# Two wide attentions of a decoder on one core: softmax sums inverted by way of DRAM, weight loads and clearing moved behind pairs

## What is computed

```python
def L0_xattn(mask, encodings, ...):      # 64 sequences, E=64, T=256, 8 heads of 8
    q, k, v = split(mask.T @ w_in.T + b_in)
    scores = q k^T / sqrt(8), kept where |i - j| <= 64
    o = softmax(scores) v
    o = (o @ w_out.T + b_out).T
    return einsum('nit,io->not', relu(o) * encodings, w_ct) + b_ct

def L1_xattn(q, k, v):                   # k = v = the context, q = layernorm(x)
    return softmax(q_h^T k_h / sqrt(8)) v_h      # 8 heads of 8, 256 x 256 scores
```

## Time and profile before

| | |
|---|---|
| median of 3 runs | 2706.45 us (2706.38 to 2707.54) |
| the profiled execution's own time, its span | 2692.82 us, 2690.8 us |
| mean granted TensorE clock | 0.914 |
| busy: PE, DVE, ACT, POOL | 2236.3, 1829.1, 1153.3, 892.3 us |
| first wide attention | about 373 to 1021 us |
| causal attention | about 1423 to 1733 us |
| second wide attention | about 1747 to 2290 us |

### The profile page before, as it was taken

How to read it: one execution, slowest core, us unless ns; L and a number is a source line. 1 busy time by engine, 2 the same in 40 slices (tenths; PEclk the granted TensorE clock), 3 DMA queues, 4 the chain that set the end, 5 groups by cost and what they waited for, 6 DMA issues and landing times. The chain is left out here.

```text
span 2690.8 us, 54881 instructions
## 1 busy us (share of the span) xinstructions
PE 2236.3 (83%) x19596; PEld 1624.8 (60%) x19596; DVE 1829.1 (68%) x4630; ACT 1153.3 (43%) x2616; POOL 892.3 (33%) x1488
## 2 busy tenths in 40 slices
PE   3777839999999991999976999669999999369795
PEld 3666726777777761899965777435555554336463
DVE  4999966777777768455544666468888886325355
ACT  1222215555555552222214666336666666123231
POOL 3555542222222213566650000133233231224422
PEclk9888859999999995999988999769999999589998
DMA  4000033333333320000012000253433432023524
GB/s 114 1 0 1 1 96 80 96 94 89 97 86 99 87 61 0 2 2 2 2 52 103 2 2 1 66 131 110 116 110 110 118 110 57 35 70 95 171 93 159
DMA packets 252300, 183.14 MB, mean 68 GB/s; under 512 B 29056, under 2 KB 246304, under 8 KB 251264
## 3 DMA queue, kind: packets, MB, share of 16 engines
q1 hardware_dynamic: 240416, 156.52, 21.0%
q0 software_dynamic: 7456, 18.92, 2.0%
q10 hardware_dynamic: 4160, 4.19, 0.5%
HBM read 94.47 MB, written 83.51 MB: 66 GB/s over the span
## 5 line engine op out<-in xcount | busy, mean ns | idle before, releaser
L780 ACT ACTIVATE xattn_pr<-ps 128x384 f32<-128x384 f32 (+1 forms) x1024 | 536.5, 541 | 383.8 <-PE ps L510 225.4
L651 DVE TENSOR_REDUCE xattn_mx<-ps 128x2 f32<-128x512 f32 (+1 forms) x768 | 464.7, 634 | 172.7 <-PE ps L495 91.8
L492 PE MATMUL ps<-xattn_kp,xattn_qp 96*128 96x192 bf16 (+1 forms) x2048 | 396.1, 265 | 47.6 <-DMA xattn_kp<-xattn_rows 21.8
L507 PE MATMUL ps<-xattn_qp,xattn_kp 128*128 128x192 bf16 (+1 forms) x2048 | 410.6, 262 | 6.0 <-ACT xattn_pr L780 4.0
L525 PE MATMUL ps<-xattn_pr,xattn_vs 128*32 128x256 f32 (+1 forms) x4096 | 308.0, 373 | 0.2
L507 PEld LDWEIGHTS ps<-xattn_qp,xattn_kp 128*128 128x128 bf16 x2048 | 181.1, 98 | 147.3 <-ACT xattn_pr L780 68.8
L492 PEld LDWEIGHTS ps<-xattn_kp,xattn_qp 96*128 96x128 bf16 x2048 | 191.3, 99 | 92.4 <-issue 30.7
L510 PE MATMUL ps<-xattn_band,xattn_ident 128*128 128x192 bf16 x1024 | 210.5, 246 | 0.0
L1018 PE MATMUL ps<-ffn_parts,gate_up_t 128*128 128x128 bf16 x3072 | 193.8, 220 | 2.1 <-DVE ffn_parts L1136 2.1
L1018 PEld LDWEIGHTS ps<-ffn_parts,gate_up_t 128*128 128x128 bf16 x3072 | 183.7, 98 | 16.4 <-DVE ffn_parts L1136 2.5
L855 POOL TENSOR_TENSOR xattn_rest<-xattn_qk,xattn_parts 128x512 f32<-128x512 f32 x64 | 74.1, 1158 | 343.0 <-ACT xattn_parts L803 343.0
(11 more groups left out here) (306 smaller groups left out, 4637.5 us busy)
## 6 DMA issues: line engine op xcount, KB each, us to landing
xattn_rows<-xattn_parts SPq DMA_DIRECT2D x128, 192.0 KB, 2.1
xattn_qp<-xattn_rows SPq DMA_DIRECT2D x256, 96.0 KB, 2.8
xattn_kp<-xattn_rows SPq DMA_DIRECT2D x256, 96.0 KB, 3.1
xattn_rows<-xattn_parts SPq DMA_DIRECT2D x128, 128.0 KB, 2.1
moe_rows_in<-region_zero SPq DMA_DIRECT2D x6, 1677.0 KB, 7.4
moe_xb<-moe_rows_in SPq DMA_DIRECT2D x78, 129.0 KB, 2.1
xattn_rows<-xattn_parts SPq DMA_DIRECT2D x128, 64.0 KB, 1.8
moe_row<-moe_rows_out SPq DMA_DIRECT2D x16, 512.0 KB, 8.3
```

Of the source, the lines that this page charges most:

```text
L492: mm = nc.tensor.matmul(out, qp[u][s][0:R_MAX, h, mt * P:(mt + 1) * P], kp[u][s][0:R_MAX, h, lo:lo + width], start=True, stop=not by_product)
L507: mm = nc.tensor.matmul(out, kp[u][s][:, h, nt * P:(nt + 1) * P], qp[u][s][:, h, lo:lo + width], start=True, stop=not banded)
L651: ins = nc.vector.tensor_reduce(mx[s][:, h * NT:(h + 1) * NT], of, AX.X, ALU.max)
L780: nc.scalar.activation(out, src, ACT.Exp, scale=HD ** -0.5).then_inc(exped, 1)
```

## The change

The values matmul now has the ones in one column of its own for each head, so the sums of 16 heads by 256 queries are eight rows of the kept outputs, and nothing is multiplied eightfold. The order of the heads in the placed operands changes with it (`TURN`). ACT starts a store of the whole kept outputs, 256 KB, to DRAM (`store_outputs`, at j = 2). SP loads the sums from there as 128 partitions by 32 (`load_sums`, 16 KB, behind the first four placements). DVE inverts them (`invert`, at j = 8). POOL stores the inverses (`store_inverses`) and loads them back with each head repeated over eight partitions (`load_inverses`, 128 KB). `normal_o` stands at j = 13 and waits for that load. PE's `align` has only the two matmuls of the outputs. In the first attention the gate product moves to j = 15, and `gate_by_context`, `out_product` and `new_x` of a pair go to the next step; there also the mask is added by matmul for 4 heads of 16 instead of 8, and by DVE's fused instruction for 12 instead of 8. The copy of the values is four DVE instructions instead of two. The memsets of kp are made as f32 words, and the first pair's store waits for half of them.

`begin_loads` is gone: POOL issues one weight load at the end of each step from step 2 on. `clear_regions` is a class now, whose memset, copies and transfers are made by POOL inside the causal attention's steps 2, 5, 9 and 13. On POOL the two left-overs of a pair are parted, and the inverses' store and load stand ahead of the first and of the second.

```diff
-            return h % 2 == 1
+            return h % 4 == 3
...
+                def load_sums(p):
+                    sp.wait_ge(o_stored, 16 * (p + 1))
+                    wait(sp, inverted, p)
+                    src = o_rows.rearrange("(g r) x -> g r x", g=QUAD)[:, SUM_ROW:SUM_ROW + 2, :].rearrange("g r (k i) -> g r k i", i=NHS * D // P)
+                    sp.dma_start(sums[:], src).then_inc(sums_in, 16)
 
...
                         load_context(p + 3, 1 - u)
                     if there(p + 2):
                         place(p + 2, u, 0)
+                    if not first:
+                        load_sums(p - 1)
                     if not last:
                         place_maxima(p + 1, 1 - u, 0)
...
                     if there(p + 2):
                         place(p + 2, u, 1)
-                    if banded and not last:
-                        load_context(p + 1, 1 - u)
+                    if banded and not first:
+                        load_context(p, u)
                 load_context(0, 0)
                 if not banded:
                     load_context(1, 1)
                 sp.wait_ge(preset, 1)
...
-                def align(p, quarter):
-
-                    sums, half = 1 - quarter // 2, quarter % 2
-                    if quarter == 0:
-                        pe.wait_ge(o_kept, p + 1)
-                        wait(pe, normal, nth(p - 1, 3, 3))
-                    at = C_SELECT + (2 * sums + half) * P
-                    mm = nc.tensor.matmul(ps[:, BANK_N, sums * D:(sums + 1) * D], c[:, at:at + P], o_sb[:, half, :],
-                                          start=(half == 0), stop=(half == 1))
-                    if half == 1:
-                        mm.then_inc(aligned, 1)
+                def align(p):
+                    pe.wait_ge(o_kept, p + 1)
+                    wait(pe, normal, p)
+                    for half in range(2):
+                        at = C_SELECT + half * P
+                        mm = nc.tensor.matmul(ps[:, BANK_N, 0:D], c[:, at:at + P], o_sb[:, half, :],
+                                              start=(half == 0), stop=(half == 1))
+                    mm.then_inc(aligned, 1)
...
-                        if j in ALIGNED and not first:
-                            for half in range(2):
-                                align(p - 1, 2 * ALIGNED.index(j) + half)
+                        if j == ALIGNED and not first:
+                            align(p - 1)
...
-                        if banded and not first and j == 11:
+                        if banded and not first and j == 15:
                             gate_product(p - 1)
-                        if banded and not first and j == 13:
-                            out_product(p - 1)
+                        if banded and p >= 2 and j == 3:
...
-                def reciprocal_sums(p, half):
-
-                    v.wait_ge(aligned, nth(p, 2, 2))
-                    wait(v, normal, nth(p - 1, 3, 3))
-                    x = slice(half * P, (half + 1) * P)
-                    nc.vector.reciprocal(rden[:, x], ps[:, BANK_N, D + half * P:D + (half + 1) * P]).then_inc(normal, 1)
+                def invert(p):
+
+                    v.wait_ge(sums_in, 16 * (p + 1))
+                    wait(v, inv_stored, 16 * p)
+                    nc.vector.reciprocal(inv[:], sums[:]).then_inc(inverted, 1)
 
                 def normal_o(p):
 
-                    v.wait_ge(normal, nth(p, 3, 2))
+                    v.wait_ge(aligned, p + 1)
+                    v.wait_ge(inv_in, 16 * (p + 1))
...
-                        if j in (7, 8) and not first:
-                            reciprocal_sums(p - 1, j - 7)
-                        if j == 9 and not first:
+                        if j == 8 and not first:
+                            invert(p - 1)
+                        if j == 13 and not first:
                             normal_o(p - 1)
-                        if j == 11 and not first and not banded:
+                        if j == 15 and not first and not banded:
                             new_x(p - 1, 1 - u)
-                        if j == 11 and not first and banded:
-                            gate_by_context(p - 1, 1 - u)
-                        if j == 14 and not first and banded:
-                            new_x(p - 1, 1 - u)
+                        if j == 1 and p >= 2 and banded:
+                            gate_by_context(p - 2, u)
+                        if j == 5 and p >= 2 and banded:
+                            new_x(p - 2, u)
...
-                    wait(a, aligned, nth(p, 2, 0))
+                    wait(a, aligned, p)
+                    wait(a, o_stored, 16 * p)
                     nc.scalar.activation(o_sb[:].rearrange("p a b -> p (a b)"), ps[:, BANK_O, :], ACT.Copy).then_inc(o_kept, 1)
+
+                def store_outputs(p):
+                    a.wait_ge(o_kept, p + 1)
+                    wait(a, sums_in, 16 * p)
+                    a.dma_start(o_rows, o_sb[:].rearrange("p a b -> p (a b)")).then_inc(o_stored, 16)
 
...
+                        if j == 2 and not first:
+                            store_outputs(p - 1)
...
             def _(g):
-                def left_overs(p, u):
+                def store_inverses(p):
+                    g.wait_ge(inverted, p + 1)
+                    wait(g, inv_in, 16 * p)
+                    g.dma_start(inv_rows.rearrange("h (k i) -> (h k) i", i=NHS * D // P), inv[:]).then_inc(inv_stored, 16)
+
+                def load_inverses(p):
+                    g.wait_ge(inv_stored, 16 * (p + 1))
+                    wait(g, normal, p)
+                    src = inv_rows.rearrange("h (a x) -> h a x", a=1).broadcast_to([NHS, HD, D])
+                    g.dma_start(rden[:], src).then_inc(inv_in, 16)
...
                         split_maxima(p + 1, 0)
+                    if not first:
+                        store_inverses(p - 1)
                     if there(p + 3):
-                        left_overs(p + 3, 1 - u)
+                        first_left_over(p + 3, 1 - u)
+                    if not first:
+                        load_inverses(p - 1)
+                    if there(p + 3):
+                        second_left_over(p + 3)
                     if not last:
                         split_maxima(p + 1, 1)
-                    if not first:
+                    if not banded and not first:
                         fin.reciprocal_std(nc, g, p - 1)
+                    if banded and p >= 2:
+                        fin.reciprocal_std(nc, g, p - 2)
+                    if 0 <= p - LATER_FROM < len(later_loads):
+                        to, of = later_loads[p - LATER_FROM]
+                        g.dma_start(to, of).then_inc(later_landed, 16)
                 for u in range(2):
                     for s in range(S2):
...
                         fin.reciprocal_std(nc, g, p - 1)
+                    if p == 2:
+                        regions.zeros(nc, g)
+                    if p >= 5 and (p - 5) % 4 == 0 and (p - 5) // 4 < regions.parts:
+                        regions.clear(nc, g, (p - 5) // 4)
                 over(g, PAIRS, step)
                 fin.reciprocal_std(nc, g, PAIRS - 1)
...
-            landed = begin_loads(core, "ternary_landed", loads)
-
-
-            wide_attention(core, "xattn0", i['ctx_2048'], wide)
+            landed = nc.alloc_semaphore(name="ternary_landed")
+
+
+            wide_attention(core, "xattn0", i['ctx_2048'], wide, later=(loads, landed))
             core.end_stage()
```

159 lines of the change are left out of this document (86 added, 73 removed).

## The result

The changed kernel takes **2945.19 us** (median of 4, 2941.05 to 2958.9) against 2706.41 (4 runs of the kernel before): a ratio of 1.0889, 95% interval 1.0868 to 1.091. I had forecast 2817 us in a range of 2700 to 2885. The sign was right, the size was not: +239 us instead of +111. The profiled execution took 2958.9 us (span 2956.9), the slowest of the four, and that of before (2692.8) was 13.7 us faster than its own median.

What follows compares the result with a forecast made beforehand. PE was taken to bound both attentions. Stage changes -40, loads +10, second attention +126, first +3 and ends +12 summed to +111, giving 2817 us from the median 2706.45, in a range of 2700 to 2885.

Steps and rivals of the forecast that it cites:

- Second attention, the chain: Second attention: sums and inverses hold up POOL, ACT, then PE, which waits 3.8 us; step 2.3 us longer.
- The clock: Second attention: PE's lowered clock behind its wait costs 2.2 us a step, between 0 and 2.9.
- Rival B: Second attention: PE's stall comes without a clock loss; 2730 to 2755 us; chance 0.22.
- Later loads: Weight loads on POOL's queue in both attentions: 32 us of transfer at worst, a third taken, +10 us.
- First attention: First attention: PE's saving returns as a wait too short to lower the clock; +0.1 us a step, +3.
- Rival D: Both attentions: POOL's transfers land slowly, as the 6.4 us at the kernel's start; above 3150 us; chance 0.06.
- Ends: End of each attention: store and load landings before the last normal_o add 6 us, twice, +12.
- Changes of stage: Three changes of stage: blocks of transfers go, taking 39.7 us of DVE's standing with them; -40.
- PE's savings: Each step: 0.93 us from two fewer alignment matmuls; first attention also 0.67 from 8 fewer mask products.

Runs made afterwards that it cites:

- e1: The changed kernel, but in the second attention POOL does the first left-over ahead of the inverses' store: 2853.6 us.
- e2: The changed kernel, but ACT stores only the 8 rows of sums instead of the whole 256 KB of outputs: 2929.6 us.
- e4: The changed kernel with eight unread matmuls on PE ahead of the score that waits for ACT in the second attention: 2883.3 us.
- e3: The kernel before plus only moved weight loads, clearing within causal attention, f32 memsets and one head in four masked by a product; sums inverted as before: 2658.1 us.
- e9: The changed kernel, POOL's queue kept: first attention, inverses' store and load ahead of both left-overs; second, first left-over ahead of them: 2801.3 us.
- e6: The changed kernel with the inverses' store and load issued by SP, behind the maxima's rows, instead of POOL: 2721.2 us.
- e10: e4 plus five such unread matmuls ahead of the first attention's gate product: 2854.5 us.
- e15: e3 with the experts' weights loaded by SP in a block of their own ahead of the second attention, as before: 2666.8 us.
- e14: e3 with the regions cleared in a block of their own ahead of causal attention, as before: 2678.1 us.
- e13: The changed kernel with inverses by SP, the sums' load ahead of the first placements, and only the 8 rows of sums stored: 2647.1 us.
- e11: e3 with every second head masked by a product, as before the change: 2668.8 us.
- e16: The changed kernel with inverses by SP and the sums' load ahead of the first placements, outputs still stored whole: 2659.2 us.
- e8: The changed kernel with inversion, scaling, products and alignment deferred to later places, and the inverses' store and load issued by SP: 2698.7 us.
- e12: e3 plus the four transfers of every pair at the same sizes, their results used by nothing: 2691.5 us.
- e17: e13 with the weight loads issued in every third step instead of every one: 2645.2 us.

## Why the prediction was wrong, point by point

The step that failed is the first attention, which I had put at +3 us and which cost 79.9. Behind it come two terms that had the right mechanism and too small a size, the second attention and the weight loads in it.

- **Second attention, the chain (+2.3 a step): right.** Every link of the step at 2219.54 lies within 0.7 us of the forecast, and e1 shows that POOL's order was what ended last. I had not seen that DVE's own waits stood right behind it (e1 kept 18.8 us, not 16). In the median the first placement is also later, 6.4 us after the copy instead of the 4.95 of before; the outputs' store may make up to 1 of it (e2). My chain started from the placements of the earlier trace rows, at t 5.8, which was one of the quick steps: the median of before is 6.6, and the change's 7.7. That is likely part of why the median step is 21.0 us and not the forecast's 20.1.
- **The clock (+2.2 a step): right**, 2.1 by e4. Rival B falls.
- **Later loads (+10): mis-sized.** In the second attention the six steps from the fourth copy on took 26.7, 27.0, 27.4, 27.2, 24.5 and 26.6 us, where others take about 21.2: 32 us. In e3, with no chain, the same steps cost 9. In these six the first placement went out 9.5 to 11.7 us after the copy. My bounds (0 to 32) held it, my third did not. The reason I gave, that the rows' store heads the new chain, was the one to trust.
- **First attention (+3): the step that failed.** It cost 79.9 us. I let the inverses' load follow the left-over and took that as 0.7 us of delay. In fact the left-over waits for ACT's rounding, which moved with PE, so the load went out 1.7 us later than forecast in the step shown; it landed in 3.8 us, not in the 2.4 of other POOL transfers; and the wait of 2.9 us was followed by the low clock. I had ruled that out here for a wait of 1.6 "by the rows above", which show only waits of 3.3 and 4.1 us with a low clock behind them and some 0.6 a step without; none of the rows lies between. By e9 the order is 1.9 us a step, by e6 the queue 1.0 (21.3, 19.3, 18.3), each with its part of the clock, which alone is 0.8 to 1.2 (e10 against e4 and against the change). Rival D had the right mechanism for a part, a slow POOL queue, at a price several times too high.
- **Ends (+12): half.** The chain of landings is there (at 2521.05 and 2530.56 DVE had waited 4.8 and 4.7 us for the inverses), and another 5.2 us each for the barrier (e6). Nothing in the trace of before had a transfer of POOL's shortly ahead of an attention's end.
- **Changes of stage (-40): right.** DVE's idle time at the three fell by 3.5, 24.0 and 11.8 us, 39.3 together. The rest of the table's -47.5 is mostly -3.1 and -7.5 from an attention's start to its first copy, for which I had no term. In the second attention 7 of the 7.5 are the experts' loads, which no longer stand ahead of the context (e15), and not the faster presets; in the first no run separates the two. Causal attention took 3.0 us longer, but the kernels that clear there range over 309 to 314 us (309.2 in e3), and the two that do not take 309.3 (before) and 307.6 (e14), so no price of the clearing is shown beyond that spread.
- **PE's savings.** 0.93 a step for the alignment shows nearly whole in e13 (14.8 against 15.6); 0.67 for the masks was 0.4 (e11).
- **Routed experts (+17.5): no term, and perhaps no effect.** All kernels with the moved half have a stage of 411 to 422 us. PE stands 2 to 6 us some six times there, ahead of the down product, mostly released by nothing that the profile names; the longest two of the changed kernel:

```profile
2722.13 1.35 PEld L1685 LDWEIGHTS ps<-expert_d,moe_ht 128*128 128x128 f32 x4 [4.44 <-issue]
...
2761.70 0.96 PEld L1685 LDWEIGHTS ps<-expert_d,moe_ht 128*128 128x128 f32 x4 [3.96 <-issue]
```

The 399.2 of before come from one execution, which was 13.7 us faster than that kernel's median. Its other stretches are like those of the kernels with the same code there: ternary MLP 374.7 us (374.6 to 376.0 in the others), causal attention 309.3, the second attention's ordinary step 15.6. So the 13.7 us should lie in the experts' stage, and then some 4 of the 17.5 are left, within the spread of that stage. The medians bear it out: e3's execution is 51.6 us ahead of before's when the experts' stage begins, and its median is 48.3 below. With 17.5 us lost in that stage it could be only 34. A second profile of the kernel before would settle it; there is none.

By size: of the 155 us between the sum made for the profiled execution (+111) and its +266, the first attention is some 75, the second some 60 (25 of it the loads), the ends 11, the experts 17 (most of it perhaps from that one execution of before), less 8 for the rest.

## What to carry to other kernels

A transfer chain that replaces a cheap instruction cost little here by its bytes (16 us in e2, 12 in e16) and much by its place: look for each instruction that stands behind a wait on its engine's queue, for the wait behind that one too, and shorten the chain (another queue, fewer bytes, ahead of the big transfers) until it ends before anyone asks. Here that took the kernel from 8.9% slower to 2.0% faster than before, but the other half of the change alone gives 1.85% (e3): even the short chain gained only 5 to 11 us. Giving the transfers that someone waits for to SP's queue instead of POOL's was worth 80 us (e6 against e9), as long as nothing urgent stood behind their waits on SP (e8). A stall on PE had two prices, its length and the slow clock behind it, and products that compute nothing took back most of the second. And a single profiled execution can be unlike its kernel's median, so compare its stages with those of other kernels that share the code.

## What the runs showed of the hardware

- POOL's transfers: 0.63 us of POOL's own time to issue the store against 0.35 on SP (the load 0.54 against 0.60), legs 0.5 us longer in the mean (e9, e6), and a barrier behind which DVE waits 8.0 us instead of 2.8 when the block ends with them (the change, e12 against e6, e3).
- Idle products keep the clock: 0.81 to 0.96 in the second attention (e4), 0.93 to 1.00 in the first (e10), worth 91 us.
- A load of 1 MB makes a step that contains a chain of small transfers 3.4 to 6.9 us longer, whether they come in each step or in each third (e13, e17), and one without such a chain 0 to 3.4 us (e3).
- The Trainium skill (DMA: Bandwidth & Descriptors, Anatomy of one DMA) has a transfer that GpSimd issues take 2.0 us and its bytes over 436 GB/s. POOL's 16 KB store fits it: issued at 2230.96, its landing let the load go at 2233.03. For SP's transfers, to which my forecast applied it, the section gives no figure, and they lie on both sides of it here: the same store by SP let the load go after a median of 1.45 us (e6), and the sums' load, with 384 KB of placements just ahead of it, was issued at 2227.57 and inverted at 2230.31, 2.7 us.
